# Four of the heaviest node tiles of a graph kernel change places with four light ones

## The chip, the core and the metric

The kernel runs on one core of one Trainium2 chip. The metric is device time in microseconds (us) of one execution. The engines are named as in the profile: PE (TensorE, matmul), DVE (VectorE), ACT (ScalarE), POOL (GpSimd, which here issues the indirect gathers) and SP (SyncE, which issues plain DMAs).

## What is computed

A graph of 6250 nodes with 256 features each and 100,000 edges passes through four residual layers. Cut to what matters:

```
x = x + relu(GAT(layernorm(x)))         # 8 heads; softmax over a node's incoming edges
x = x + relu(MoE32(layernorm(x)))       # one of 32 small experts for each node
x = x + segment_sum((layernorm(x) @ W[edge_type])[src] * edge_weight, dst)   # 16 relations
x = x + layernorm(mix of 2 of 8 experts(layernorm(x)) + layernorm(x))
```

The edges are sorted by destination, so a node's incoming edges stand together; their number is the node's degree. The largest degree in the inputs is 32.

## The kernel before

Nodes are worked in 49 tiles of 128. A tile's edges are fetched column by column: one indirect gather on POOL brings, for each of 128 nodes, the row of its j-th edge, so a tile needs as many gathers as the largest degree in it (and eight at least). To waste few of them, the first stage (`search_and_project`) sorts the nodes by degree: it counts them in bins of degree (L397 to L420), and from a node's rank its tile is `rank_high` (the rank divided by 128, L423) and its row in the tile is `rank_low` (L424). Tile 0 is the lightest and tile 48 the heaviest. All later stages take tiles in this order.

The number of gathers of each tile, from the degrees in the inputs:

| tiles | gathers each |
|---|---|
| 0 to 8 | 8, 9, 10, 11, 11, 11, 12, 12, 12 |
| 9 to 16 | 13, 13, 13, 13, 14, 14, 14, 14 |
| 17 to 26 | 15 (five times), 16 (five times) |
| 27 to 38 | 17 (five times), 18 (four times), 19 (three times) |
| 39 to 44 | 20, 20, 20, 21, 21, 22 |
| 45 to 48 | 22, 23, 25, 32 |

They add up to 799, once in each of two stages.

`attention` works tiles in pairs (2i, 2i+1); tile 48 is alone. For a tile, POOL gathers a window of edge keys (L788), the rows (L812) and the node's own record (L818). DVE makes a mask (L1176), waits until all gathers have landed, makes the scores (L1181 to L1186), and waits for ACT's exponentials (L855). Then it weighs and adds the rows, `items` steps of four columns (L1212 and L1217, with L1232 the last), and releases the buffer (`summed`). The row buffer holds 48 columns for two tiles of up to 32 each: POOL may begin tile t when tile t-2 is summed, and column 16 of tile t when tile t-1 is. PE works behind this: the small experts of pair i-2 and the relation projections of pair i-4. ACT works all of it in one written order (`pair`, from L931): it evacuates two projection chunks (L905, `tr_row`), makes the exponentials of the even tile, evacuates further chunks, does four of the eight expert steps (L896, `mo_ht`), makes the exponentials of the odd tile, and goes on. So whatever of PE's output comes behind a late exponential in this order waits for it.

`relations` gathers again (L1444), now rows of the projected table, and DVE adds them one column at a time in PSUM (L1639 and L1640, in steps of four columns) after it has released the next indices (L1649). Beside it PE works the eight dense experts of tiles 0 to 27 in seven groups of four, and the other 21 tiles are left to the last stage, `feed_forward`, which has no gathers and is alike for all tiles.

Of the kernel before, what the change touches and what calls it, by code (L numbers as in the profile page):

```python
# [16 lines left out]
F32 = mybir.dt.float32  # L17
BF16 = mybir.dt.bfloat16
I32 = mybir.dt.int32
U32 = mybir.dt.uint32  # L20
ALU = mybir.AluOpType
# [3 lines left out]
P = 128  # L25
N_NODES, N_EDGES, D = 6250, 100000, 256
NT = -(-N_NODES // P)
# [69 lines left out]
def spread(ap, axis, shape):  # L97

    return ap.unsqueeze(axis).broadcast_to(shape)
# [79 lines left out]
def search_and_project(p: Program):  # L179
# [3 lines left out]
    PARTS = U  # L183
    NEXT_AT, COUNT_AT, ORDER_AT = 27, 31, 37
    FIELDS = 3
    CELLS = DBINS * NT
    CB = CELLS // 4
    with p.phase() as ctx:
        def sb(n, s, d):
            return ctx.enter_context(nc.sbuf_tensor(n, s, d))  # L190
# [7 lines left out]
        chunk_i = sb("chunk_i", [P, NT], I32)  # L198
        shared = sb("shared", [P, NT * FIELDS * NT], F32)
        found = shared[:, 0:NT * P].bitcast(I32).rearrange("q (t e) -> q t e", e=P)  # L200
        valued = shared[:].rearrange("q (t f h) -> q t f h", f=FIELDS, h=NT)
        cmp = sb("cmp", [P, NT, P], BF16)
# [6 lines left out]
        ranked = sb("ranked", [P, DBINS, NT], F32)  # L209
        base = sb("base", [P, 4, DBINS], F32)  # L210
        rank = sb("rank", [P, NT], F32)
        rank_i, rank_high, rank_low = (sb(n, [P, NT], I32) for n in ("rank_i", "rank_high", "rank_low"))
        rank_row = sb("rank_row", [P, NT, HT - HROW], F32)
        fields = sb("fields", [P, NT, FIELDS], F32)
        hot_high = p.win[:].rearrange("q t c -> q (t c)")[:, 0:NT * NT].rearrange("q (t h) -> q t h", h=NT)
# [23 lines left out]
        high_ready, row_ready, low_ready, valued_ready, ordered = (  # L239
            p.sem(x) for x in ("high_ready", "row_ready", "low_ready", "valued_ready", "ordered"))  # L240
# [45 lines left out]
        def _(pool):  # L286
# [27 lines left out]
            for k in range(PARTS):  # L314
                lo, hi = k * U, (k + 1) * U
                pool.wait_ge(high_ready, k + 1)
                pool.tensor_tensor(valued[:, lo:hi], spread(hot_high[:, lo:hi, :], 2, [P, U, FIELDS, NT]),
                                   spread(fields[:, lo:hi, :], 3, [P, U, FIELDS, NT]), ALU.mult).then_inc(valued_ready, 1)

# [7 lines left out]
        def _(dve):  # L327
            chain = Chain(p, dve, steps_v)
# [89 lines left out]
            chain(ins)  # L418
            chain(dve.tensor_tensor(ranked[:], ranked[:], hot[:], ALU.mult))
            chain(dve.tensor_reduce(rank[:], ranked[:].rearrange("q b t -> q t b"), AX, ALU.add))  # L420
            dve.tensor_copy(rank_row[:, :, 0], rank[:]).then_inc(row_ready, 1)
            chain(dve.tensor_copy(rank_i[:], rank[:]))
            chain(dve.tensor_scalar(rank_high[:], rank_i[:], bits, None, ALU.arith_shift_right))  # L423
            chain(dve.tensor_scalar(rank_low[:], rank_i[:], P - 1, None, ALU.bitwise_and))  # L424

            for k in range(PARTS):
                lo, hi = k * U, (k + 1) * U
# [7 lines left out]
            dve.wait_ge(ordered, 1)  # L435
            chain(dve.tensor_copy(p.info[:].rearrange("q f t -> q (f t)"), p.bank[4][:, 0:FIELDS * NT]))
            dve.sem_inc(info_ready, 1)
# [1659 lines left out]
def build(nc, a):  # L2097
    with ExitStack() as ctx:
        p = Program(nc, ctx, a)
        search_and_project(p)  # L2100
        attention(p)
        p.rec = p.keep("rec", [P, max(DONE, TAIL), D], F32)
        relations(p)
        p.gb = p.keep("gb", [P, 2, D], F32)
        p.xd = [p.keep(f"xd{n}", [P, G, D], F32) for n in range(2)]
        p.x3 = [p.keep(f"x3{n}", [P, G, D], F32) for n in range(2)]
        choose_two(p)
        feed_forward(p)
# [33 lines left out]
```

## Time and profile before

| | us |
|---|---|
| median of 3 runs (3031.24 to 3037.5) | 3033.62 |
| the profiled execution's own time | 3030.64 |
| its span, first to last instruction | 3028.8 |
| PE busy | 2529.5 (84%) |
| POOL busy | 1947.3 (64%) |
| DVE busy | 1785.2 (59%) |
| ACT busy | 906.6 (30%) |

By the trace's order of instructions the stages lie about so: `search_and_project` to 141 us, `attention` from there to about 1788, `relations` from about 1793 to 2820, and the choice of two experts and `feed_forward` from there to the end. Shares of the whole span say little, since the stages have different limits; each is read by itself.

### The profile page before, as it was taken

To read this page: it belongs to the slowest core of one execution; us is meant where nothing else is said; L and a number is where in the kernel's file an instruction comes from. 1 tells how busy PE (TensorE), PEld (TensorE's weight loads), DVE (VectorE), ACT (ScalarE), POOL (GpSimd) and SP (SyncE) were. 2 spreads that over 40 slices of the span, in tenths; PEclk is the share of its full clock that TensorE was granted. 3 is DMA by queue.
4 is the path that set the end of the run, shared out by engine and by line. 5 is a ranking of instruction groups with operands and counts; after the bars stand their busy time and mean duration, and the time that the engine had idled before them with its cause. 6 is when DMAs were issued, how large, how long until landed. Compare 5 with 4: busy or idle time off the path is not lost. (4 is left out here: it accounts for less than half of the span.)

```text
span 3028.8 us, 39157 instructions
## 1 busy us (share of the span) xinstructions
PE 2529.5 (84%) x9508; PEld 1701.3 (56%) x9508; DVE 1785.2 (59%) x4152; ACT 906.6 (30%) x1799; POOL 1947.3 (64%) x1892
## 2 busy tenths in 40 slices
PE   4626999999999999998869953999999999940497
PEld 3515666666666666665546622666666666630265
DVE  6867665656566766666652016665556555444688
ACT  2312343334333433333223321333333333300321
POOL 6377746665667777787750027777777777776255
PEclk9858999999999999999989976999999999965699
DMA  7463545455545555555541265555556455443332
GB/s 247 115 191 93 149 143 150 137 157 151 152 141 165 163 157 156 164 171 153 153 123 70 82 218 183 152 156 156 150 155 184 143 147 150 142 121 99 123 123 69
DMA packets 257283, 443.01 MB, mean 146 GB/s; under 512 B 51178, under 2 KB 148066, under 8 KB 257186
## 3 DMA queue, kind: packets, MB, share of 16 engines
q0 software_dynamic: 84608, 232.41, 28.9%
q1 hardware_dynamic: 136626, 176.53, 16.9%
q10 hardware_dynamic: 35952, 33.04, 3.3%
q8 instruction: 29, 0.48, 0.1%
q14 instruction: 68, 0.56, 0.1%
HBM read 275.36 MB, written 166.45 MB: 146 GB/s over the span
## 5 line engine op out<-in xcount | busy, mean ns | idle before, releaser
L812 POOL DMA_INDIRECT gat_rows<-h_table,idx x799 | 902.9, 1130 | 374.9 <-issue 235.7
L1444 POOL DMA_INDIRECT rel_rows<-transformed,rel_idx x799 | 755.3, 945 | 468.0 <-issue 460.8
L1056 PE MATMUL bank<-tr_wr,tr_xt 128*128 128x512 f32 x1568 | 722.9, 601 | 51.1 <-ACT tr_row L905 46.2
L1056 PEld LDWEIGHTS bank<-tr_wr,tr_xt 128*128 128x128 f32 x1568 | 297.0, 192 | 334.0 <-issue 270.5
L905 ACT ACTIVATE tr_row<-bank 128x512 f32<-128x512 f32 x392 | 233.6, 597 | 661.5 <-PE bank L1056 636.2
L1499 PE MATMUL bank<-ex_xt,ex_w 128*128 128x512 f32 x896 | 420.2, 596 | 8.6 <-ACT ex_ht L1575 7.1
L1640 DVE SCALAR_TENSOR_TENSOR bank<-rel_rows,rel_now,bank 128x256 f32<-128x256 f32 x823 | 403.2, 490 | 40.3
L1021 PE MATMUL bank<-mo_xt,mo_w 128*128 128x256 f32 (+1 forms) x1600 | 408.9, 379 | 19.4 <-ACT mo_ht L896 17.7
L1508 PE MATMUL bank<-ex_w,ex_ht 128*128 128x256 f32 x1792 | 420.7, 380 | 0.0
L1508 PEld LDWEIGHTS bank<-ex_w,ex_ht 128*128 128x128 f32 x1792 | 341.6, 191 | 129.1 <-issue 93.6
L1039 PE MATMUL bank<-mo_w,mo_ht 128*128 128x256 f32 x1568 | 368.9, 381 | 5.3 <-ACT mo_ht L896 5.3
L1021 PEld LDWEIGHTS bank<-mo_xt,mo_w 128*128 128x128 f32 x1600 | 287.0, 193 | 111.3 <-issue 57.9
L1039 PEld LDWEIGHTS bank<-mo_w,mo_ht 128*128 128x128 f32 x1568 | 299.6, 191 | 55.5 <-issue 11.0
L1212 DVE TENSOR_TENSOR gat_rows<-gat_rows 128x1024 f32<-128x1024 f32 (+1 forms) x169 | 254.7, 1531 | 111.4 <-DVEq L1203 111.2
L1499 PEld LDWEIGHTS bank<-ex_xt,ex_w 128*128 128x128 f32 x896 | 171.1, 191 | 142.2 <-issue 121.3
L1575 ACT ACTIVATE ex_ht<-bank,ex_b 128x512 f32<-128x512 f32 x224 | 153.2, 686 | 275.6 <-ACTq L1574 275.6
L896 ACT ACTIVATE mo_ht<-bank,mo_b 128x256 f32<-128x256 f32 (+1 forms) x400 | 164.9, 464 | 229.2 <-PE bank L1021 198.2
L1217 DVE TENSOR_TENSOR gat_rows<-gat_rows 128x1056 f32<-128x1056 f32 x169 | 212.0, 1255 | 1.7
L1583 ACT ACTIVATE ex_y<-bank 128x256 f32<-128x256 f32 x224 | 85.8, 383 | 232.2 <-ACTq L1582 232.2
L1649 DVE CAST rel_idx<-win 128x32 int32 (+1 forms) x49 | 12.1, 246 | 216.2 <-DMA rel_rows<-transformed,rel_idx 213.2
L1532 PE MATMUL bank<-ms,rec 128*128 128x1 f32 x84 | 14.8, 308 | 137.3 <-DVEq L1723 97.9
L1181 DVE TENSOR_TENSOR gat_score<-gat_rows,gat_x 128x256 f32<-128x256 f32 x49 | 30.6, 625 | 140.7 <-DMA gat_rows<-h_table,idx 122.1
(296 smaller groups left out, 2252.4 us busy)
## 6 DMA issues: line engine op xcount, KB each, us to landing
transformed<-tr_row SPq DMA_DIRECT2D x392, 256.0 KB, 2.3
ys<-ex_y ACTq DMA_DIRECT2D x224, 128.0 KB, 2.0
gat_rows<-h_table,idx POOLq DMA_INDIRECT x799
rel_rows<-transformed,rel_idx POOLq DMA_INDIRECT x799
ex_w<-L_ffn_W SPq DMA_DIRECT2D x16, 512.0 KB, 12.1
ff_ye<-ys SPq DMA_DIRECT2D x14, 512.0 KB, 7.4
h_table<-hrow SPq DMA_DIRECT2D x49, 132.0 KB, 2.6
records<-xa SPq DMA_DIRECT2D x49, 132.0 KB
```

The source lines that it names most:

```text
L812: pool.indirect_dma_start(out=rows[:, column(u, j), :], out_offset=None, in_=p.h_table[:], in_offset=bass.IndirectOffsetOnAxis(ap=idx[u][: ...
L896: ins = act.activation(ht[:, b % HALF, 0:n * P], p.bank[2 + k % 2][:, h * PT:h * PT + n * P], ACT.Relu, bias=b1[:, b:b + 1])
L905: act.activation(trow[c % SLOTS_T][:], p.bank[6 + c % 2][:], ACT.Copy).then_inc(evacuated, 1)
L1021: ins = pe.matmul(to[h], w1[:, kd, b * P:(b + 1) * P], xt[:, kd, 0:n * P], start=(h == 0 and kd == 0), stop=(h == 1 and kd == KD - 1))
L1039: ins = pe.matmul(p.bank[4 + u][:, 0:D], ht[:, b % HALF, u * P:(u + 1) * P], w2[:, b, :], start=(b == 0), stop=False)
L1056: ins = pe.matmul(p.bank[6 + c % 2][:], xt2[:, k, u * P:(u + 1) * P], wr[:, k, m * CW:(m + 1) * CW], start=(k == 0), stop=(k == KD - 1))
L1212: dve.tensor_tensor(m[:, :, :, 0:HEAD_DIM], m[:, :, :, 0:HEAD_DIM], m[:, :, :, HEAD_DIM:HW].broadcast_to([P, COLS[s], HEADS, HEAD_DIM]), A ...
L1217: dve.tensor_tensor(total, total, columns(u, JCOL, 2 * JCOL) if s == 0 else part(s), ALU.add).then_inc(summing, 1)
L1444: pool.indirect_dma_start(out=rows[:, column(u, j), :], out_offset=None, in_=p.transformed[:], in_offset=bass.IndirectOffsetOnAxis(ap=idx[ ...
L1499: ins = pe.matmul(p.bank[3 + n % 2][:], w1[:, e, k, f * P:(f + 1) * P], xt[:, k, :], start=(k == 0), stop=(k == KD - 1))
L1508: ins = pe.matmul(p.bank[5 + m % 3][:, 0:D], ht[:, e % 2 * F + f, j * P:(j + 1) * P], w2[:, e * F + f, :], start=(f == 0), stop=(f == F - 1))
L1640: return dve.scalar_tensor_tensor(total, row, w, total, ALU.mult, ALU.add)
```

## The change

The tile number of a node is changed after the sort, so the node keeps its row in the tile. With `HEAVIEST` 4 and `SPREAD_AT` 9, tiles 45, 46, 47 and 48 change places with tiles 15, 13, 11 and 9: `step_` is 105 - 3h for tile number h; a heavy tile (h of 45 or more) moves by that, and a light one (odd, 9 to 15) by half of it. The odd member of pairs 4, 5, 6 and 7 is now a heavy tile. In the order of the program the gathers of each tile now are:

| tiles | before | after |
|---|---|---|
| 8, 9 | 12, 13 | 12, 32 |
| 10, 11 | 13, 13 | 13, 25 |
| 12, 13 | 13, 14 | 13, 23 |
| 14, 15 | 14, 14 | 14, 22 |
| 44, 45 | 22, 22 | 22, 14 |
| 46, 47 | 23, 25 | 14, 13 |
| 48 | 32 | 13 |

```diff
+    HEAVIEST, SPREAD_AT = 4, 9
...
-        rank_i, rank_high, rank_low = (sb(n, [P, NT], I32) for n in ("rank_i", "rank_high", "rank_low"))
+        rank_i, rank_high, rank_low, rank_odd = (sb(n, [P, NT], I32) for n in ("rank_i", "rank_high", "rank_low", "rank_odd"))
+        tile_at = sb("tile_at", [P, 4, NT], F32)
...
             chain(dve.tensor_reduce(rank[:], ranked[:].rearrange("q b t -> q t b"), AX, ALU.add))
-            dve.tensor_copy(rank_row[:, :, 0], rank[:]).then_inc(row_ready, 1)
             chain(dve.tensor_copy(rank_i[:], rank[:]))
             chain(dve.tensor_scalar(rank_high[:], rank_i[:], bits, None, ALU.arith_shift_right))
             chain(dve.tensor_scalar(rank_low[:], rank_i[:], P - 1, None, ALU.bitwise_and))
+            moved_to, step_, light, heavy = (tile_at[:, n, :] for n in range(4))
+            chain(dve.tensor_scalar(rank_odd[:], rank_high[:], 1, None, ALU.bitwise_and))
+            chain(dve.tensor_copy(moved_to, rank_high[:]))
+            chain(dve.tensor_scalar(step_, moved_to, -3.0, float(2 * NT + SPREAD_AT - 2), ALU.mult, ALU.add))
+            chain(dve.scalar_tensor_tensor(light, moved_to, float(SPREAD_AT), rank_odd[:], ALU.is_ge, ALU.mult))
+            chain(dve.scalar_tensor_tensor(light, moved_to, float(SPREAD_AT + 2 * HEAVIEST - 2), light, ALU.is_le, ALU.mult))
+            chain(dve.scalar_tensor_tensor(heavy, moved_to, float(NT - HEAVIEST), step_, ALU.is_ge, ALU.mult))
+            chain(dve.scalar_tensor_tensor(light, light, 0.5, step_, ALU.mult, ALU.mult))
+            chain(dve.tensor_tensor(moved_to, moved_to, light, ALU.add))
+            chain(dve.tensor_tensor(moved_to, moved_to, heavy, ALU.add))
+            chain(dve.tensor_copy(rank_high[:], moved_to))
+            chain(dve.scalar_tensor_tensor(rank[:], moved_to, float(P), rank_low[:], ALU.mult, ALU.add))
+            dve.tensor_copy(rank_row[:, :, 0], rank[:]).then_inc(row_ready, 1)
```

On DVE, at the end of the sort in the first stage, before the change (`ranked` and `rank` are the rank in float, `rank_row` its copy for the table that SP stores, `win` and `hot_low` the one-hot masks for PE, `xn` a normed tile of the projection):

```order
L419 TENSOR_TENSOR ranked<-ranked,hot 128x1568
L420 TENSOR_REDUCE rank<-ranked 128x49
L421 COPY rank_row<-rank 128x49
L422 CAST rank_i<-rank 128x49
L423 TENSOR_SCALAR rank_high<-rank_i 128x49
L424 TENSOR_SCALAR rank_low<-rank_i 128x49
L428 TENSOR_TENSOR win<-rank_high,count 128x343
L430 TENSOR_TENSOR hot_low<-rank_low,count 128x896
```

and after it, from the tile number on:

```order
L424 TENSOR_SCALAR rank_high<-rank_i 128x49
L425 TENSOR_SCALAR rank_low<-rank_i 128x49
L429 TENSOR_SCALAR rank_odd<-rank_high 128x49
L430 CAST tile_at<-rank_high 128x49
L431 TENSOR_SCALAR tile_at<-tile_at 128x49
L432 SCALAR_TENSOR_TENSOR tile_at<-tile_at,rank_odd 128x49
...
L438 CAST rank_high<-tile_at 128x49
L439 SCALAR_TENSOR_TENSOR rank<-tile_at,rank_low 128x49
L440 COPY rank_row<-rank 128x49
L444 TENSOR_TENSOR win<-rank_high,count 128x343
L446 TENSOR_TENSOR hot_low<-rank_low,count 128x896
```

Eleven small chained instructions have come between the tile number and the masks, and the copy to `rank_row` stands behind them. On PE, ACT, POOL and SP the rows are the same in both programs but for line numbers; there it is the loops' counts that change, since they are read from a table made on the chip. So for each tile in `attention`, POOL's rows stand as

```order
L788 DMA w_buf<-pairs,w_at 128x64
L804 REGISTER_ALU
L812 DMA gat_rows<-h_table,idx 128x268 x8
L818 DMA gat_x<-records,w_at 128x264
L583 COMPARE_AND_BRANCH
L812 DMA gat_rows<-h_table,idx 128x268
```

in both, with a branch and one further gather (L583, L812) for each column above eight, up to the tile's count. What moves is how often the last two repeat at a place, as the table says.

## Rows read from the trace of the kernel before

**Rows 1.** Busy time by engine (instructions), granted clock, DMA: the middle of `attention`.

```profile
core 0: us, PE busy (x) PEld busy (x) DVE busy (x) ACT busy (x) POOL busy (x), PEclk, DMA share, GB/s
286.00:1280.00 994.00, 991.87 (x3834) 668.90 (x3833) 628.68 (x1254) 358.03 (x690) 673.98 (x603) 1.00 0.52 151
```

**Rows 2.** Timeline of PE, end of `attention`: start, us, instructions, [idle before <-releaser].

```profile
1467.81 3.60 PE L1056 MATMUL bank<-tr_wr,tr_xt 128*128 128x512 f32 x8
...
1488.84 6.78 PE L1056 MATMUL bank<-tr_wr,tr_xt 128*128 128x512 f32 x8 [8.93 <-ACT tr_row L905]
...
1528.24 1.13 PE L1021 MATMUL bank<-mo_xt,mo_w 128*128 128x256 f32 x4 [1.14 <-ACT mo_ht L896]
...
1577.81 6.67 PE L1056 MATMUL bank<-tr_wr,tr_xt 128*128 128x512 f32 x8 [23.97 <-ACT tr_row L905]
```

**Rows 3.** Timeline of ACT: exponentials of tiles 9, 10, 11, 12, 46 and 47.

```profile
347.37 0.67 ACT L855 ACTIVATE gat_rows<-gat_score 128x256 f32<-128x256 f32 x1
...
380.94 0.67 ACT L855 ACTIVATE gat_rows<-gat_score 128x256 f32<-128x256 f32 x1 [0.49 <-issue]
...
407.49 0.67 ACT L855 ACTIVATE gat_rows<-gat_score 128x256 f32<-128x256 f32 x1 [0.19 <-issue]
...
440.86 0.67 ACT L855 ACTIVATE gat_rows<-gat_score 128x256 f32<-128x256 f32 x1 [0.44 <-issue]
...
1487.69 0.67 ACT L855 ACTIVATE gat_rows<-gat_score 128x256 f32<-128x256 f32 x1 [10.47 <-DVE gat_score L1186]
...
1526.93 0.67 ACT L855 ACTIVATE gat_rows<-gat_score 128x256 f32<-128x256 f32 x1 [10.30 <-DVE gat_score L1186]
```

**Rows 4.** POOL's gathers of L812 alone, one stretch per tile: tiles 9, 47, 48.

```profile
313.00:333.00 20.00, 13.75 (x13) 1.00 0.66 194
...
1484.40:1522.20 37.80, 28.16 (x25) 0.86 0.61 175
1523.60:1571.90 48.30, 36.45 (x32) 0.84 0.43 119
```

**Rows 5.** Timeline of DVE: end of tile 9, mask of 10, scores and end of 47.

```profile
357.46 0.43 DVE L1232 TENSOR_TENSOR gat_acc<-gat_rows 128x264 f32<-128x264 f32 x1
...
363.05 0.24 DVE L1176 TENSOR_SCALAR gat_mask<-gat_place,info 128x32 f32<-128x32 f32 x1 [2.10 <-issue]
...
1524.15 0.62 DVE L1181 TENSOR_TENSOR gat_score<-gat_rows,gat_x 128x256 f32<-128x256 f32 x1 [8.90 <-DMA gat_rows<-h_table,idx]
...
1544.54 0.51 DVE L1232 TENSOR_TENSOR gat_acc<-gat_rows 128x264 f32<-128x264 f32 x1
```

**Rows 6.** Timeline of POOL and DVE as DVE begins to weigh a tile's rows.

```profile
1452.86 0.94 POOL L812 DMA_INDIRECT gat_rows<-h_table,idx  x1 [0.30 <-issue]
...
1456.34 2.00 POOL L812 DMA_INDIRECT gat_rows<-h_table,idx  x1 [0.30 <-issue]
1457.44 1.22 DVE L1212 TENSOR_TENSOR gat_rows<-gat_rows 128x1024 f32<-128x1024 f32 x1
```

**Rows 7.** POOL's gathers of L1444 alone: tile 48 of `relations`, and the whole stage.

```profile
2755.40:2795.30 39.90, 30.23 (x32) 0.50 0.37 105
1793.50:2795.30 1001.80, 755.34 (x799) 0.90 0.52 155
```

**Rows 8.** Timeline of `relations`: a held gather; adds of tiles 11 and 48; tile 12's start.

```profile
1844.29 0.94 POOL L1444 DMA_INDIRECT rel_rows<-transformed,rel_idx  x1 [2.18 <-DVEq L1693]
...
1968.06 8.03 DVE L1640 SCALAR_TENSOR_TENSOR bank<-rel_rows,rel_now,bank 128x256 f32<-128x256 f32 x15
...
1985.53 0.19 DVE L1649 CAST rel_idx<-win 128x32 int32 x1 [0.29 <-DVE rel_now L1645]
...
2797.74 16.80 DVE L1640 SCALAR_TENSOR_TENSOR bank<-rel_rows,rel_now,bank 128x256 f32<-128x256 f32 x31
```

**Rows 9.** Timeline of DVE and PE where the tile numbers are made.

```profile
100.31 0.19 DVE L423 TENSOR_SCALAR rank_high<-rank_i 128x49 int32<-128x49 int32 x1
100.53 0.19 DVE L424 TENSOR_SCALAR rank_low<-rank_i 128x49 int32<-128x49 int32 x1
...
104.26 0.69 PE L490 MATMUL bank<-ident,xn 128*128 128x128 f32 x2 [6.14 <-DVE xn L372]
```

## The prediction, made before the changed kernel was run

> **What bounds the kernel now.** The columns of busy time over the whole span mix stages, so I read stretch by stretch, and only the three stages that the change reaches: the end of the sort, `attention` and `relations`.
>
> The middle of `attention` belongs to PE. In 994 us PE is busy for 991.9, at the full granted clock (1.00, the 2.4 GHz level), while POOL's gathers fill 674 [rows 1]. A pair of tiles takes 60 us there: the exponentials of tiles 10 and 12 stand at 380.9 and 440.9, and ACT meets them without waiting for DVE [rows 3]. So a gather may come later there at no cost until ACT has to wait for it, and PE behind ACT.
>
> The end of `attention` belongs to POOL. A gather costs about 1.25 us from start to start (39.9 us for 32 where nothing disturbs it) [rows 7]; the stretches of tiles 47 and 48 take 37.8 and 48.3 us [rows 4], so with their windows and records pairs 23 and 24 need far more than 60 us of POOL. What ends PE's idle time there is ACT, and ACT waits for the scores: 10.47 us before the exponentials of tile 46, 10.30 before those of tile 47 [rows 3]. PE loses 8.93, 1.14 and 23.97 us [rows 2].
>
> `relations` belongs to POOL all along: 799 gathers in 1001.8 us, that is 1.25 each from the first to the last, with almost nothing between [rows 7]. PE's dense experts end long before it does (the last two stretches run at the lower clock). Here the order of tiles can't shorten the gathers, only make or remove waits between them and change what follows the last one.
>
> **The change, part by part.** *Longer sort.* Eleven chained DVE instructions come in front of the masks, of the size of those beside them, which start 0.22 us apart [rows 9]: 11 x 0.22 = +2.4 us. No cover: PE waits 6.14 us for DVE right behind [rows 9]. The copy to `rank_row` only changes place, and SP asks for it only behind tile 38 of the projection, whose `xn` DVE makes after the masks. Tiles and rows are otherwise the same, so all plain DMAs and matmuls are too.
>
> *The end of attention.* Tiles 45 to 48 now have 14, 14, 13 and 13 gathers. With 1.25 us each, plus window, record and a few slowed ones, a pair needs some 40 us of POOL, under the 60 of PE, as today's pairs 5 to 8 do, for which ACT doesn't wait [rows 3]. So the idle time behind tiles 46, 47 and 48 goes: 8.93 + 1.14 + 23.97 = 34.0. PE's first eight matmuls after the two long waits take 6.78 and 6.67 us where such a group takes 3.60 [rows 2]; those 3.2 and 3.1 go too. Together -40.3 us. Waits behind tiles up to 44 stay, since those tiles keep their gathers and so POOL its lateness.
>
> *The middle of attention.* Now heavy tiles stand in pairs 4 to 7, and I follow lateness through them. Two prices first. For an odd tile PE has work in hand when ACT stops: behind tile 47 ACT waited 10.30 us [rows 3] and PE lost 1.14 [rows 2], so 9.2 us are covered. For an even tile hardly any: behind tile 46 ACT waited 10.47 and PE lost 8.93 and 3.2 by slower matmuls, the wait plus 1.6.
>
> - Tile 9, 32 gathers for 13. Its gathers start at 313.0 and end at 333.0 [rows 4]; nineteen more at 1.25 end at about 356.6. From there to the scores it is 2 us (1522.2 to 1524.15 for tile 47) [rows 4, 5], and scores to exponentials take 2.8 (1524.15 to 1526.93) [rows 3, 5]: 361.4. ACT is there at 347.4, so it waits 14.0, and PE loses 14.0 - 9.2 = 4.8. Bounds: 0 if the stretch were shortened by more overlap, 9.7 if it took tile 48's whole 48.3 us.
> - Tile 10. DVE weighs tile 9 in seven steps; tile 47 with six took 18.1 us from exponentials to the end of L1232 (1526.93 to 1545.05) [rows 3, 5], so 18.1 x 7/6 = 21.1, ending at 382.5. Mask 5.2 later (357.89 to 363.05) [rows 5], exponentials 3.2 after the mask: 390.9. ACT, shifted by 4.8, is there at 380.45 + 4.8 = 385.2 [rows 3]. It waits 5.6, and PE loses 5.6 + 1.6 = 7.2.
> - Tile 11, 25 gathers, may start when tile 9 is summed, 383.4; with tile 47's 37.8 us [rows 4] its exponentials are ready at 383.4 + 37.8 + 4.8 = 426.0. ACT is there at 407.3 + 12.0 = 419.3, waits 6.7, under the 9.2: no loss.
> - Tile 12: 426.0 + 18.1 + 5.2 + 3.2 = 452.5, against ACT at 440.4 + 12.0 = 452.4: none. Tile 13 with 23 gathers starts at 445 and needs two gathers fewer than tile 47, so its exponentials are ready at 445 + 35.3 + 4.8 = 485.1; ACT is there 26.5 us behind tile 12, as at tiles 10 and 11, at 479: a wait of 6, no loss. Pairs 7 and on have regained their time.
>
> Together +12.0 us. Ends: 5 if PE's work in hand covers all of tile 9 and part of tile 10, and 29 if that stock isn't refilled after the first stall, so that tiles 11 and 13 cost their 6.7 and 6 too and tile 9's gathers take the upper bound.
>
> One row bears on the gathers' price. A gather that runs while DVE weighs rows takes 2.00 us instead of 0.94 [rows 6], so tile 47's stretch is longer than 25 x 1.25; the heavy tiles of the middle meet the short weighing of light neighbours, so I took today's stretch of tile 9 plus undisturbed gathers. The Trainium skill ("SBUF — State Buffer", section "Who interferes with whom") says that a `tensor_tensor` with two SBUF inputs contends only with GpSimd's reads and infers that descriptor generation isn't held up by it. By that a gather beside L1212 would stay at 0.94, tile 9's 33 issues would take some 41 us (an estimate from that page and 1.25 us each) and the whole come out 2 us lower; the row differs, and the sum goes by the row.
>
> *Relations.* The gathers keep their total. New waits: tile t may start when t-2 is summed, and a light even tile is now too short to cover a heavy odd one. Tile 9: from its last gather to DVE's adds 2.4 us (2795.3 to 2797.7) [rows 7, 8], 31 adds 16.8 us, then 2.2 until POOL goes on (a held gather waited 2.18) [rows 8], 21.4; tile 10's 13 gathers cover 16.3: POOL waits 5.1. Tile 11: 27 adds at 0.54, in all 19.2 against 16.3: 2.9. Tiles 13 and 15: 17.1 against 17.5: none. Sum +8.0. After the last gather tile 48 now has 15 adds instead of 31: 16 x 0.54 = -8.7. But DVE will begin them some 2 us later than today: it needs 9.4 us from the last add of an odd tile to the next even one (1976.1 to 1985.5) [rows 8], so with 2.4 + 8.1 us for tile 47 it is ready 19.9 us behind that tile's last gather, while 13 gathers take 16.3: the adds begin 3.6 + 0.6 instead of 2.4 behind the last gather, +1.8. In all +1.1 us; the ends are -7 (waits hidden) and +8 (no gain at the end).
>
> **Sum:** +2.4 - 40.3 + 12.0 + 1.1 = -24.8 us on the profiled execution's 3030.6, 3005.8. The median lies 3.0 us above that execution; on it, 3033.6 - 24.8 = 3008.8.
>
> **Rivals.** *More is hidden in the middle* (5 for 12, with relations at its lower end): -24.8 - 7 - 7, from 2995 to 3002. For it: POOL has about a third of the middle free [rows 1]. Against: that time can't be used ahead, since POOL may be only one tile in front of DVE.
>
> *PE's stock isn't refilled*: 29 for 12, so 3026, between 3019 and 3031. For it: the waits of tiles 11 and 13, 6.7 and 6, lie near the 9.2. Against: ACT is busy for 358 of 994 us where PE is full [rows 1], so it works about three times as fast as PE feeds it and catches up within a few steps.
>
> *Slower: the extra gathers aren't hidden at all.* Pairs 4 to 7 get 19 + 12 + 9 + 8 = 48 more gathers, 60 us. If each stands in front of ACT as at the end of the stage today, +60 takes the place of +12: 3033.6 + 2.4 - 40.3 + 60 + 1.1 = 3057. It decides against the change from 37 us of loss in these four pairs. For it: they come right behind the stage's start-up, with no lead. Against: by the steps above the second two heavy tiles find ACT late anyway.
>
> *The change doesn't move the tiles*: only the eleven instructions remain, 3036. The arithmetic of the new tile numbers gives whole numbers and the pairs listed, so hardly likely.
>
> **How the numbers follow.** Forecast 0.62, more hidden 0.12, stock not refilled 0.16, slower 0.07, not moved 0.03. The forecast's time is 3009. Eight in ten: from 2997, the middle of the better case, to 3024, which takes in the upper price of tile 9 and much of the third case. About 0.2% (6 us) is what a measurement of this kernel can tell from no change, so faster means under 3027.5: 0.62 + 0.12 + two thirds of 0.16, 0.84; within 0.2%: the rest of the third case and the last, 0.09; slower 0.07.
>
> **What would show it.** In the changed trace, POOL's stretches of 32 and 25 gathers stand at about 315 and 385 us. PE's timeline has idle time of about 5 us behind `mo_ht` at 360 and about 6 behind `tr_row` at 390, none over 2 us until tile 40, and none over 2 us behind the last four tiles. In `relations` POOL waits once for about 5 and once for about 3 us near tiles 11 and 13, and the last run of adds has 15. It is wrong if ACT waits over 15 us before tile 11 or 13, if PE still idles behind the last tiles (then it is DVE, not POOL, that is late there), or if gathers in the middle cost clearly more than 1.25 us.

## The result, and the profile after

| | before | after |
|---|---|---|
| median of 4 runs each, side by side | 3035.25 (3031.24 to 3037.5) | 3016.08 (3015.09 to 3017.26) |
| the profiled execution, its span | 3030.64, 3028.8 | 3016.06, 3014.2 |

The ratio is 0.9934, with a 95% interval of 0.9922 to 0.9946: the change makes the kernel 0.7% faster. The forecast was 3009.

Where the time went stands in the start times of a few rows of each trace: the first gather of `attention`, the exponentials of tiles 26 and 44, the first and the last gather of `relations`, the end of the router's matmuls (L1532 of before). The columns are the stretches between them, in us. The two columns "again" are second profiles of the same two kernels, from the experiments; two profiles of one kernel differ by 3 to 5 us in all, so a difference of 1 or 2 us in a stretch says nothing.

| stretch | before | before again | after | after again | predicted change |
|---|---|---|---|---|---|
| to the first gather of `attention` | 146.5 | 145.2 | 149.3 | 147.5 | +2.4 |
| to tile 26's exponentials (middle) | 714.4 | 716.0 | 730.6 | 730.2 | +12.0 |
| to tile 44's exponentials | 554.3 | 555.4 | 555.9 | 555.7 | 0 |
| to the first gather of `relations` (end of `attention`) | 378.4 | 378.4 | 337.2 | 337.2 | -40.3 |
| gathers of `relations` | 1001.6 | 1002.6 | 1014.5 | 1012.2 | +8.0 |
| from the last gather to the router's end | 25.7 | 25.6 | 17.5 | 17.5 | -6.9 |
| to the end | 207.9 | 208.8 | 209.1 | 208.8 | 0 |
| span | 3028.8 | 3032.0 | 3014.2 | 3009.0 | -24.8 |

**End of the sort.** PE's row of after that answers to [rows 9] (timeline: start, length, instructions, idle before and who ended it):

```profile
107.09 0.69 PE L506 MATMUL bank<-ident,xn 128*128 128x128 f32 x2 [8.75 <-DVE xn L374]
```

The wait has grown by 2.6 and the row stands 2.8 later.

**End of `attention`.** Busy time of the stretch (PE, PEld, DVE, ACT, POOL, then clock), and ACT's exponentials of tiles 46, 47 and 48 of after, which answer to [rows 2] and [rows 3]:

```profile
1480.00:1768.00 288.00, 278.45 (x1021) 174.47 (x1020) 66.32 (x158) 104.24 (x199) 32.51 (x31) 0.99 0.30 102
```

```profile
1498.32 0.67 ACT L871 ACTIVATE gat_rows<-gat_score 128x256 f32<-128x256 f32 x1 [0.46 <-issue]
1524.90 0.67 ACT L871 ACTIVATE gat_rows<-gat_score 128x256 f32<-128x256 f32 x1 [0.18 <-issue]
1558.12 0.68 ACT L871 ACTIVATE gat_rows<-gat_score 128x256 f32<-128x256 f32 x1 [0.28 <-issue]
```

Waits of 10.47 and 10.30 us before the exponentials are gone; ACT meets the scores ready. PE's 8.93, 1.14 and 23.97 have no row in after.

**Middle of `attention`.** The same stretch as [rows 1], 2.8 later, and a short one of PE alone behind its first wait (busy, clock, DMA share, GB/s):

```profile
288.80:1282.80 994.00, 981.99 (x3775) 659.84 (x3776) 650.05 (x1269) 353.36 (x684) 738.33 (x638) 0.99 0.54 156
```

```profile
366.00:372.00 6.00, 5.46 (x14) 0.50 0.50 159
```

PE was busy for 991.87 of 994 before and is for 981.99 now, with 59 instructions fewer in the same time. The idle time has grown by only 10 us, from 2 to 12, and for 6 us the matmuls ran at the 1.2 GHz level (0.50). PE's timeline of after shows both:

```profile
355.77 1.03 PE L1037 MATMUL bank<-mo_xt,mo_w 128*128 128x256 f32 x4
...
366.54 2.08 PE L1037 MATMUL bank<-mo_xt,mo_w 128*128 128x256 f32 x4 [5.21 <-ACT mo_ht L912]
...
376.78 1.88 PE L1072 MATMUL bank<-tr_wr,tr_xt 128*128 128x512 f32 x4
...
395.54 3.70 PE L1072 MATMUL bank<-tr_wr,tr_xt 128*128 128x512 f32 x8 [0.62 <-ACT tr_row L921]
400.24 0.28 PE L1018 MATMUL bank<-mo_identb,mo_hot 128*128 128x128 bf16 x2 [1.00 <-DVE mo_hot L1144]
401.65 2.53 PE L1072 MATMUL bank<-tr_wr,tr_xt 128*128 128x512 f32 x4 [1.12 <-ACT tr_row L921]
...
407.36 1.88 PE L1072 MATMUL bank<-tr_wr,tr_xt 128*128 128x512 f32 x4
...
464.75 1.98 PE L1072 MATMUL bank<-tr_wr,tr_xt 128*128 128x512 f32 x4 [0.97 <-ACT tr_row L921]
467.60 1.13 PE L1037 MATMUL bank<-mo_xt,mo_w 128*128 128x256 f32 x4 [0.86 <-ACT mo_ones L902]
...
469.64 1.88 PE L1072 MATMUL bank<-tr_wr,tr_xt 128*128 128x512 f32 x4
```

The group that starts at 366.54 takes 2.08 us where the same group before the wait took 1.03. To see what all this costs, I count PE's matmuls of a line and take the same ones in before. Four of the rows above (355.77, 376.78, 407.36, 469.64) are these of before:

```profile
352.25 1.02 PE L1021 MATMUL bank<-mo_xt,mo_w 128*128 128x256 f32 x4
...
364.98 1.88 PE L1056 MATMUL bank<-tr_wr,tr_xt 128*128 128x512 f32 x4
...
390.23 1.88 PE L1056 MATMUL bank<-tr_wr,tr_xt 128*128 128x512 f32 x4
...
450.21 1.88 PE L1056 MATMUL bank<-tr_wr,tr_xt 128*128 128x512 f32 x4
```

PE is late by 3.5 us ahead of tile 9's wait, 11.8 behind it, 17.1 behind tile 10's, 19.4 behind tile 12's, and stays there: a matmul near 600 us is also 19.4 late. So tile 9 costs 8.3, tile 10 5.3, tiles 11 and 12 2.3, and the rest nothing: 15.9 in all. The sum holds in the second profile of after, but its parts move. By the same count it is 15.4 there, of which tile 9 costs 5.9, tile 10 5.5 and tile 12 4.0. Tile 9's row is this one:

```profile
363.57 2.08 PE L1037 MATMUL bank<-mo_xt,mo_w 128*128 128x256 f32 x4 [4.11 <-ACT mo_ht L912]
```

PE came to this wait 1.9 us less late than in the first profile, tile 9's exponentials stood 3.0 us earlier, and the clock was back sooner (0.94 between 366 and 372 us).

ACT in the same stretch: the exponentials of tiles 9, 10, 11 and 12 (L871), and two evacuations (L921) that wait for something else:

```profile
365.23 0.67 ACT L871 ACTIVATE gat_rows<-gat_score 128x256 f32<-128x256 f32 x1 [14.38 <-DVE gat_score L1202]
...
394.23 0.68 ACT L871 ACTIVATE gat_rows<-gat_score 128x256 f32<-128x256 f32 x1 [1.99 <-DVE gat_score L1202]
...
401.00 0.60 ACT L921 ACTIVATE tr_row<-bank 128x512 f32<-128x512 f32 x1 [5.03 <-DMA transformed<-tr_row]
...
430.79 0.68 ACT L871 ACTIVATE gat_rows<-gat_score 128x256 f32<-128x256 f32 x1 [6.36 <-DVE gat_score L1202]
...
457.75 0.68 ACT L871 ACTIVATE gat_rows<-gat_score 128x256 f32<-128x256 f32 x1 [0.20 <-issue]
...
464.10 0.60 ACT L921 ACTIVATE tr_row<-bank 128x512 f32<-128x512 f32 x1 [3.12 <-DMA transformed<-tr_row]
```

ACT waits 5.03 and 3.12 us not for scores but for a store of an earlier chunk to leave its buffer. SP issues the x store of pair i-3 (L781) in front of the chunk stores of pair i-4 (L787), and the x store waits for DVE; when DVE is late with a heavy tile, ACT's four `tr_row` buffers are held through SP's queue. SP's timeline has no chunk store between 387.25 and 398.19:

```profile
397.40 0.42 SPq L781 DMA_DIRECT2D x_moved<-tr_x  x1
398.19 12.37 SPq L787 DMA_DIRECT2D transformed<-tr_row  x8
```

A late DVE also reaches PE directly, by the one-hot mask `mo_hot` (1.00 at 400.24).

**`relations`.** All gathers as one stretch (POOL busy, clock, DMA share, GB/s), POOL's three longest waits between gathers that before does not have, and DVE's last run of adds:

```profile
1773.00:2787.60 1014.60, 758.31 (x799) 0.89 0.52 153
```

```profile
1957.86 0.95 POOL L1460 DMA_INDIRECT rel_rows<-transformed,rel_idx  x1 [5.16 <-DVEq L1709]
2008.42 0.95 POOL L1460 DMA_INDIRECT rel_rows<-transformed,rel_idx  x1 [3.21 <-DVEq L1709]
2319.05 0.95 POOL L1460 DMA_INDIRECT rel_rows<-transformed,rel_idx  x1 [2.38 <-issue]
...
2790.45 8.03 DVE L1656 SCALAR_TENSOR_TENSOR bank<-rel_rows,rel_now,bank 128x256 f32<-128x256 f32 x15
```

Against [rows 7] the gathers take 12.8 more: two waits for DVE (5.16 and 3.21, less the usual 0.30 each), 7.8; one of 2.1 that waits for nothing in the profile, at the second gather of tile 28; and 3.0 because a gather took 949 ns on the mean instead of 945. The last run of adds has 15 and starts 2.9 us behind the last gather's end (2787.6), where it was 2.5 before.

### The profile page after: what moved, and what is told of

The parts are those of the page before. It is cut to its first block and busy times, and to the rows that moved or that the text cites. A ratio compares the mean times of both kernels' runs of the same rounds, so it can differ in the third digit from the quotient of the medians.

```text
span 3014.2 us, 39170 instructions
## 1 busy us (share of the span) xinstructions
PE 2536.2 (84%) x9508; PEld 1702.3 (56%) x9508; DVE 1784.8 (59%) x4163; ACT 907.8 (30%) x1799; POOL 1972.8 (65%) x1892
## 5 line engine op out<-in xcount | busy, mean ns | idle before, releaser
L828 POOL DMA_INDIRECT gat_rows<-h_table,idx x799 | 917.3, 1148 | 307.3 <-issue 240.0
L1037 PE MATMUL bank<-mo_xt,mo_w 128*128 128x256 f32 (+1 forms) x1600 | 416.3, 384 | 22.1 <-ACT mo_ht L912 19.4
L921 ACT ACTIVATE tr_row<-bank 128x512 f32<-128x512 f32 x392 | 233.9, 598 | 662.5 <-PE bank L1072 632.3
L1656 DVE SCALAR_TENSOR_TENSOR bank<-rel_rows,rel_now,bank 128x256 f32<-128x256 f32 x823 | 403.2, 490 | 40.3
L1228 DVE TENSOR_TENSOR gat_rows<-gat_rows 128x1024 f32<-128x1024 f32 (+1 forms) x169 | 254.5, 1530 | 87.7 <-DVEq L1219 87.7
L1233 DVE TENSOR_TENSOR gat_rows<-gat_rows 128x1056 f32<-128x1056 f32 x169 | 211.7, 1252 | 1.7
L1665 DVE CAST rel_idx<-win 128x32 int32 (+1 forms) x49 | 11.8, 241 | 224.0 <-DMA rel_rows<-transformed,rel_idx 221.2
L1197 DVE TENSOR_TENSOR gat_score<-gat_rows,gat_x 128x256 f32<-128x256 f32 x49 | 30.6, 625 | 145.2 <-DMA gat_rows<-h_table,idx 127.0
## 6 DMA issues: line engine op xcount, KB each, us to landing
ex_w<-L_ffn_W SPq DMA_DIRECT2D x16, 512.0 KB, 11.4
```

The costliest lines, as they stand in the source:

```text
L828: pool.indirect_dma_start(out=rows[:, column(u, j), :], out_offset=None, in_=p.h_table[:], in_offset=bass.IndirectOffsetOnAxis(ap=idx[u][: ...
L921: act.activation(trow[c % SLOTS_T][:], p.bank[6 + c % 2][:], ACT.Copy).then_inc(evacuated, 1)
L1037: ins = pe.matmul(to[h], w1[:, kd, b * P:(b + 1) * P], xt[:, kd, 0:n * P], start=(h == 0 and kd == 0), stop=(h == 1 and kd == KD - 1))
L1228: dve.tensor_tensor(m[:, :, :, 0:HEAD_DIM], m[:, :, :, 0:HEAD_DIM], m[:, :, :, HEAD_DIM:HW].broadcast_to([P, COLS[s], HEADS, HEAD_DIM]), A ...
L1233: dve.tensor_tensor(total, total, columns(u, JCOL, 2 * JCOL) if s == 0 else part(s), ALU.add).then_inc(summing, 1)
L1656: return dve.scalar_tensor_tensor(total, row, w, total, ALU.mult, ALU.add)
```

## The experiments

**The change without its effect, and before once more.** In `sort_only` the eleven instructions run but no tile moves; `before_again` is the unchanged kernel.

```diff
-            chain(dve.scalar_tensor_tensor(light, moved_to, float(SPREAD_AT), rank_odd[:], ALU.is_ge, ALU.mult))
+            chain(dve.scalar_tensor_tensor(light, moved_to, float(2 * NT), rank_odd[:], ALU.is_ge, ALU.mult))
...
-            chain(dve.scalar_tensor_tensor(heavy, moved_to, float(NT - HEAVIEST), step_, ALU.is_ge, ALU.mult))
+            chain(dve.scalar_tensor_tensor(heavy, moved_to, float(2 * NT), step_, ALU.is_ge, ALU.mult))
```

> The eleven instructions stay, but their bounds are set so that no tile is moved. Theory A (they stand uncovered in front of the masks): the profiled span is 2.4 to 2.8 us above before, first gather of attention at 149 instead of 146.5, all else as before. Rival (the sort is covered, or moving instructions there costs more than they take): under 1 or over 5 us.

> The kernel before, unchanged, for a second profile of it. Theory A (the two profiles differ only by the change): span within 3 us of 3028.8, 799 gathers of relations in 1001 to 1003 us, no gather of the end of that stage held by POOL itself. Theory B (part of the missing 5 us is the chip or the run, not the change): the 799 gathers take 1004 us or more here too, since in the changed kernel each was some 0.004 us slower and one wait of 2 us stood in POOL's own queue.

`sort_only` took 3035.65 against 3032.56 of before beside it (ratio 1.0008, 0.9999 to 1.0017). By the times alone that is not clear of noise, but the same matmul of PE as above stands at 106.51, 2.3 later than in before, with a wait of 8.76, and the gathers of `relations` take 1001.9. `before_again` had a span of 3032.0, its gathers took 1002.6, and none was held by POOL itself, as theory A said. So the instructions cost their 2 to 3 us, and everything else in the result comes from where the tiles stand.

**One heavy tile alone.** Only tiles 48 and 9 change places.

```diff
-    HEAVIEST, SPREAD_AT = 4, 9
+    HEAVIEST, SPREAD_AT = 1, 9
```

> HEAVIEST 1: only tiles 48 and 9 change places. Theory A (the price in the middle is made by the first heavy tile, behind which all later ones are late): the middle loses 11 of the 15 us that four heavy tiles cost (5 to 6 behind tile 9, some 5 behind tile 10), the end keeps PE's waits of 9 and 1 us behind tiles 46 and 47 and loses that of 24; with -3 in relations about 16 us under before. Rival (each heavy tile costs its share, about 4 us): 22 to 24 us under before.

It took 3028.63, only 4 us under before (ratio 0.9986, 0.9977 to 0.9996): a miss for both theories. Shown are PE's wait behind tile 46, POOL's last 16 gathers in `relations`, and DVE's adds of tiles 47 and 48:

```profile
1505.14 6.60 PE L1072 MATMUL bank<-tr_wr,tr_xt 128*128 128x512 f32 x8 [9.59 <-ACT tr_row L921]
```

```profile
2773.00:2792.60 19.60, 14.97 (x16) 0.50 0.38 107
```

```profile
2778.94 14.60 DVE L1656 SCALAR_TENSOR_TENSOR bank<-rel_rows,rel_now,bank 128x256 f32<-128x256 f32 x27
...
2801.93 8.03 DVE L1656 SCALAR_TENSOR_TENSOR bank<-rel_rows,rel_now,bank 128x256 f32<-128x256 f32 x15
```

The end of `attention` became 26 us shorter and the middle 10 to 11 longer, so one tile at place 9 costs over two thirds of what four cost. But the wait behind tile 46 stays (9.59). And in `relations` the last gathers end at 2792.6 while the last run of adds starts at 2801.93: DVE's adds for tile 47 with its 25 columns end only at 2793.54, and what it does between an odd tile and the next comes behind them. So the 16 adds fewer shorten nothing much (24.0 us from the last gather to the router's end, 25.6 before), while the gathers take 1009.2. In all `relations` lost some 5 us where theory A had put a gain of 3. The gain behind the last gather needs a light tile 47 as well as a light tile 48.

**Other places.** `spread17` puts the four heavy tiles at 17, 19, 21 and 23, further from the start-up of the stage; `even16` at 16, 18, 20 and 22, so that the heavy tile is the first of its pair.

```diff
-    HEAVIEST, SPREAD_AT = 4, 9
+    HEAVIEST, SPREAD_AT = 4, 17
```

```diff
-    HEAVIEST, SPREAD_AT = 4, 9
+    HEAVIEST, SPREAD_AT = 4, 16
...
-            chain(dve.scalar_tensor_tensor(light, moved_to, float(SPREAD_AT), rank_odd[:], ALU.is_ge, ALU.mult))
+            chain(dve.scalar_tensor_tensor(light, moved_to, float(SPREAD_AT), rank_odd[:], ALU.is_ge, ALU.is_gt))
```

> SPREAD_AT 17: the same four heavy tiles, now at 17, 19, 21 and 23, where POOL has waits of its own and ACT meets scores that are long ready. Theory A (the price in the middle comes of standing right behind the start-up, where POOL has no lead): PE has no idle time over 2 us in the middle, attention 41 us shorter at its end, relations with one wait of 2 us, in all about 40 us under before, 18 to 22 under the changed kernel. Rival (a heavy tile beside a light one costs the same at any place): 15 to 22 us under before, as the changed kernel.

> The four heavy tiles at 16, 18, 20 and 22, the even members of their pairs, one place before those of spread17 (17, 19, 21, 23). Theory C (at 17 to 23 the price comes through DVE: the second half of a heavy odd tile's gathers waits until the light even tile is summed, its weighing takes 20 us, and the next even tile's scores, for which PE has hardly any work in hand, come late; a heavy even tile is followed by an odd one, for which PE has 9 us in hand): the middle loses 2 to 6 us instead of about 20, and the whole is 12 to 18 us under spread17, near 2995. Rival (a pair of heavy and light costs the same in either order): as spread17, 3011.

`spread17` took 3011.1 (0.9931, 0.9917 to 0.9944), `even16` 3007.47 (0.992, 0.9903 to 0.9937). Their middles are 735.4 and 734.8 us long, even a little longer than that of after; they regain it in `relations`, where one longer wait of POOL, 2.73 and 2.92 us, stands in place of two of 5.16 and 3.21 (gathers 1006.1 and 1006.2). So neither a place further on nor the order in a pair makes the heavy tiles free; I had expected both to. ACT's exponentials of tiles 17 to 20 in `spread17` show what goes on:

```profile
598.67 0.67 ACT L871 ACTIVATE gat_rows<-gat_score 128x256 f32<-128x256 f32 x1 [9.13 <-DVE gat_score L1202]
628.22 0.67 ACT L871 ACTIVATE gat_rows<-gat_score 128x256 f32<-128x256 f32 x1 [5.33 <-DVE gat_score L1202]
665.38 0.68 ACT L871 ACTIVATE gat_rows<-gat_score 128x256 f32<-128x256 f32 x1 [8.23 <-DVE gat_score L1202]
694.06 0.67 ACT L871 ACTIVATE gat_rows<-gat_score 128x256 f32<-128x256 f32 x1 [3.79 <-DVE gat_score L1202]
```

PE's loss by the count above is 20.9 us there: 7.6 by tiles 17 and 18, the rest behind tiles 20, 22 and 24. I read this as each heavy tile finding POOL and DVE still late from the one before; the next run tests it.

**A light pair between heavy ones.** `odd_spaced` puts them at 17, 21, 25 and 29, one to every second pair (one DVE instruction more).

```diff
-    HEAVIEST, SPREAD_AT = 4, 9
+    HEAVIEST, SPREAD_AT = 4, 17
...
-            chain(dve.tensor_scalar(rank_odd[:], rank_high[:], 1, None, ALU.bitwise_and))
+            chain(dve.tensor_scalar(rank_odd[:], rank_high[:], 3, None, ALU.bitwise_and))
+            chain(dve.tensor_scalar(rank_odd[:], rank_odd[:], 1.0, None, ALU.is_equal))
...
-            chain(dve.tensor_scalar(step_, moved_to, -3.0, float(2 * NT + SPREAD_AT - 2), ALU.mult, ALU.add))
+            chain(dve.tensor_scalar(step_, moved_to, -5.0, float(4 * (NT - 1) + SPREAD_AT), ALU.mult, ALU.add))
...
-            chain(dve.scalar_tensor_tensor(light, moved_to, float(SPREAD_AT + 2 * HEAVIEST - 2), light, ALU.is_le, ALU.mult))
+            chain(dve.scalar_tensor_tensor(light, moved_to, float(SPREAD_AT + 4 * HEAVIEST - 4), light, ALU.is_le, ALU.mult))
...
-            chain(dve.scalar_tensor_tensor(light, light, 0.5, step_, ALU.mult, ALU.mult))
+            chain(dve.scalar_tensor_tensor(light, light, 0.25, step_, ALU.mult, ALU.mult))
```

> The four heavy tiles at 17, 21, 25 and 29: still odd, but with an untouched pair between (one more small DVE instruction in the sort, 0.2 us). Theory C1 (DVE's lateness adds up over neighbouring pairs, and one light pair is enough to make it good): only the tile with 32 gathers costs, some 7 us, and the whole is 10 to 13 us under spread17. Rival C2 (each heavy odd tile costs by itself): as spread17 within 4 us.

It took 2998.31 (0.9893, 0.9876 to 0.9909), some 13 us less than after and than `spread17`, as the theory said. ACT's exponentials of tiles 17 to 20, to be read against those of `spread17`, and PE's rows behind tiles 17 and 18:

```profile
598.18 0.67 ACT L872 ACTIVATE gat_rows<-gat_score 128x256 f32<-128x256 f32 x1 [9.70 <-DVE gat_score L1203]
627.69 0.67 ACT L872 ACTIVATE gat_rows<-gat_score 128x256 f32<-128x256 f32 x1 [5.29 <-DVE gat_score L1203]
656.99 0.68 ACT L872 ACTIVATE gat_rows<-gat_score 128x256 f32<-128x256 f32 x1 [0.18 <-issue]
690.13 0.67 ACT L872 ACTIVATE gat_rows<-gat_score 128x256 f32<-128x256 f32 x1 [0.21 <-issue]
```

```profile
599.49 1.13 PE L1038 MATMUL bank<-mo_xt,mo_w 128*128 128x256 f32 x4 [0.54 <-ACT mo_ht L913]
628.84 5.40 PE L1073 MATMUL bank<-tr_wr,tr_xt 128*128 128x512 f32 x8 [3.75 <-ACT tr_row L922]
635.97 1.98 PE L1073 MATMUL bank<-tr_wr,tr_xt 128*128 128x512 f32 x4 [1.62 <-ACT tr_row L922]
```

The tile with 32 gathers costs 8.3 us of PE's time, nearly all behind the light tile that follows it; then the lateness is gone, and the tiles with 25, 23 and 22 gathers cost nothing. The middle is 722.5 us long, and the gathers of `relations` take 1004.6, with one wait of POOL behind the heaviest tile (2.75 us before tile 19) and none behind the others.

The light pair is worth the 12.9 us by which the middle is shorter than that of `spread17` (735.4). Against after the middle is only 8 us shorter, and 3 are lost again up to tile 44; another 8 to 10 us come from the gathers of `relations`, of which `spread17` has 6 to 8 already by its places (1006.1).

**The order of SP's stores.** `after_again` is the changed kernel unaltered, beside `store_later`, which issues the chunk stores in front of the x store:

```diff
             def pair(i):
-                store(i - 3)
                 store_chunks(i - 4)
+                store(i - 3)
```

> The changed kernel, with SP's store of a pair's new x put behind the chunk stores of the older pair instead of in front of them. In the profile the x store waits for DVE's finish, and the chunk stores behind it keep ACT's four chunk buffers, 5.0 us at 396 and 3.1 at 461. Theory D (this is a second way by which a late DVE holds PE, beside the exponentials): ACT's waits for the chunk stores behind tiles 10, 12, 40, 42 and 44 fall under 1 us, and the whole is 4 to 8 us under the changed kernel. Rival (what waits there is released by the exponentials in any case): within 2 us of it.

> The changed kernel, unchanged, on the chip of the other runs of this call: 0.6 to 0.7% under before; its gathers of relations show whether the 13 us more than before (8 of them waits) come again. Chip or run: within 1010 us for the 799 gathers. The change: 1013 to 1016 us.

`after_again` took 3011.8 (0.9939, 0.9922 to 0.9956), `store_later` 3009.15 (0.9927, 0.991 to 0.9943). The difference of 2.7 us lies within the intervals, under theory D's 4 to 8. `after_again` repeats the longer gathers of `relations` (1012.2). PE's rows of `store_later` that answer to those of after from 366 to 470 us:

```profile
363.77 1.13 PE L1037 MATMUL bank<-mo_xt,mo_w 128*128 128x256 f32 x4 [2.75 <-ACT mo_ht L912]
...
392.75 5.39 PE L1072 MATMUL bank<-tr_wr,tr_xt 128*128 128x512 f32 x8 [3.38 <-ACT tr_row L921]
...
456.13 3.70 PE L1072 MATMUL bank<-tr_wr,tr_xt 128*128 128x512 f32 x8 [1.44 <-ACT tr_row L921]
460.97 0.28 PE L1018 MATMUL bank<-mo_identb,mo_hot 128*128 128x128 bf16 x2 [1.14 <-DVE mo_hot L1144]
```

ACT has no wait for a chunk store left there, and PE's loss in the middle, counted as above, is 11.4 instead of 15.4 to 15.9. But that is hardly the store order's doing. Tile 9 costs 2.9 us here, all of it idle time, where it cost 5.9 in `after_again`; no chunk store is waited for ahead of it in either, and PE simply came to it 1.5 us later. Tile 10 costs 5.5 in both, and tile 12 3.0 instead of 4.0. The wait for late scores grows in place of the other (3.38 where 0.62 and, in `after_again`, 1.89 stood), and behind tile 12 PE waits for `mo_hot` (1.14). So the queue does hold ACT, but what it held back is late by DVE's other ways too: as far as these runs show, the rival is right.

**More of it.** `spaced_six` spreads the six heaviest tiles as `odd_spaced` does four (the edit is against `odd_spaced`); `spaced_store` is `odd_spaced` with the order of `store_later`; `spaced_six_store` has both.

```diff
-    HEAVIEST, SPREAD_AT = 4, 17
+    HEAVIEST, SPREAD_AT = 6, 17
```

> The change with the six heaviest tiles (43 to 48) in places 17, 21, 25, 29, 33 and 37, one to every second pair: tile 48 to place 17, tile 47 to 21, and so on down to tile 43 in place 37. Theory (a place costs only where it gets many more gathers than its neighbours and has no light pair behind it; the end costs because heavy tiles stand in neighbouring pairs): places 33 and 37 get 5 and 3 more gathers each and cost nothing, and in the last pairs PE's wait of 6.3 us that odd_spaced still has at 1430 us goes, with its slow matmuls; waits at 1293 and 1360 stay, since tiles 40 to 42 keep their gathers. So 7 us under odd_spaced, 2991, with the stretch from tile 44's exponentials to the first gather of relations unchanged. Rival (each tile moved into the middle takes from PE's stock what it gives back at the end): within 3 us of odd_spaced, 2995 to 3001, with new waits of PE behind tiles 33 to 40.

> odd_spaced with SP's order of store_later: the projection chunks go into SP's queue ahead of the x store. Theory D (a late DVE holds ACT's tr_row buffers over SP's queue): the chunks wait behind the x store only where DVE is late, behind place 17 and at the end of the stage, so it gives 1 to 3 us under odd_spaced, 2995 to 2997. Rival (the waits only merge with those behind the late exponentials): no difference over 1 us, 2998.

> Both of the above. If they act at different places, the sum of both: spaced_six less 1 to 3 us, 2988 to 2990. If the order of the stores only counts where DVE is late, it gives less here than in spaced_store, under 1 us, since fewer late tiles are left at the end.

`spaced_six` took 3001.82 (0.9905, 0.9889 to 0.9922), `spaced_store` 2996.5 (0.9883, 0.9866 to 0.9899), `spaced_six_store` 3001.23 (0.9905, 0.9888 to 0.9921). These runs were timed beside other runs of before than `odd_spaced`, so the ratios are compared. The last two heavy tiles bring nothing (0.9905 against 0.9893, with intervals that overlap), as the rival said: PE's wait of 6.25 us at 1430 in `odd_spaced` is gone, but others have come, behind place 37 for instance:

```profile
1236.26 3.70 PE L1073 MATMUL bank<-tr_wr,tr_xt 128*128 128x512 f32 x8 [2.10 <-ACT tr_row L922]
```

ACT waits 4.05 and 3.64 us there before the exponentials of tiles 37 and 38, with 21 gathers in place 37, only two more than stood there (place 33 gets four more; I had written 5 and 3). That a light pair regains less among neighbours of 18 or 19 gathers than among those of 15 would explain it, but was not tried by itself. The store order takes ACT's waits for chunk stores out of `spaced_store` too, 6.05 us behind tile 18 among them, but what is left of that in the ratio, 0.1%, is less than the intervals span; with six tiles nothing is left of it. `odd_spaced` and `spaced_store` are the fastest kernels here, 1.1 to 1.2% under before, and not told apart.

## Why the prediction was right, and where it missed

The forecast of 3009 lies 7 us under the median of 3016.08, 1.6 of them because before itself took 3035.25 this time and not 3033.6. The sign of each stage is as it said, and its size within 4 us. By its own steps:

- *Sort*, +2.4: +2.8 and +2.3 in the two pairs of profiles. Right.
- *End of `attention`*, -40.3: -41.2, twice. Right, with its mechanism: POOL's pairs fit under PE's, and the slow matmuls behind the long waits go as well.
- *Middle*, +12.0: 15.9 and 15.4. This term was mis-sized, and it came as near as this because its errors went both ways.
  - Tile 9: 8.3 and 5.9 for 4.8. ACT's wait of 14.0 was 14.38, and PE's work in hand covered 9.2 of it, as forecast (5.21 idle). But I priced only the idle time. The matmuls behind it ran at the 1.2 GHz level and cost 3.1 more (8.3 less 5.21), 1.8 in the second profile (5.9 less 4.11). The price for an odd tile came from tile 47 of before, whose 1.14 us of idle time had no slow matmuls behind it [rows 2]; I had counted them for even tiles alone. How much idle time there is depends on where PE stands when the wait begins, and that moves by some 2 us from profile to profile.
  - Tile 10: 5.3 and 5.5 for 7.2. ACT waited for the scores for 1.99 us instead of 5.6, since it came later than I had it. By my price that would be 3.6; the rest came with the wait of 5.03 for a chunk store, a way from the late DVE to ACT that I had not followed.
  - Tiles 11 and 12: 2.3 and 4.0 for none. ACT's wait at tile 11 was the 6.7 forecast (6.36), covered. Behind tile 12 the scores came in time, as forecast, but SP's queue held `tr_row`. In `store_later`, where it doesn't, tile 12 costs 3.0 by late scores and a late `mo_hot`: what I put at nothing is DVE's lateness, by whichever way it comes.
  - Tile 13 and on: none, as forecast.
- *Relations*, +1.1: the second profiles give +1.5 (1012.2 + 17.5 against 1002.6 + 25.6), the first +4.7. The two waits came to 4.9 and 2.9 where 5.1 and 2.9 stood. The wait of 2.1 us in POOL's own queue comes again: at the same gather it is 2.35 long (with the usual 0.30) in the second profile and 2.40 in `store_later`, and neither profile of before has it. The 3.0 us by slower gathers are in the first profile alone. Both stay unexplained. Of the 1.8 us for a late DVE at the end, 0.4 came.

Against the second profiles the sum of -24.8 stands beside -23.0 (3032.0 to 3009.0), against the first beside -14.6; by the medians it is -19.2 in the first comparison and -18.6 in the second. About 4 us of the miss is thus the middle, shown above; the rest is spread over stretches that differ as much between two profiles of one kernel, and is left open.

Of the rivals, *stock not refilled* did not come: the waits of tiles 11 and 13 (6.36 and 4.03) were covered in full. *More is hidden* was false for these places; `odd_spaced` reaches its time, 2998. What I didn't see is that the four places were the change's weak point. At places 17 to 23 neighbouring pairs share one lateness, and a light pair between them takes 13 us off the middle; place 17 instead of 9 takes another 6 to 8 us off the gathers of `relations`. At place 9 a light pair alone was not tried; it could save little, since one heavy tile there cost 11.5 of the 15.4 to 15.9.

## What to carry to other kernels

Heavy items spread over a pipeline with slack are hidden best if each is worked off before the next comes: with four heavy tiles in neighbouring pairs the kernel gained 0.7%, with a light pair between them 1.1%. When a wait is priced, add the slower matmuls behind it to the idle time, and follow a late engine along every way on which something waits for it, the stores' too; closing one of them gained nothing clear here, because the same lateness came by the others. In a stage that sums at its end, the last two tiles count together, since the engine that sums them is behind by one.

## What the runs showed of the hardware

A gather of tile 10 that POOL issues while DVE weighs the heavy tile 9 takes 2.00 us instead of 0.95, and a heavy tile keeps that up for seven issues in a row. DVE's and POOL's timelines of after:

```profile
366.66 3.43 DVE L1228 TENSOR_TENSOR gat_rows<-gat_rows 128x2048 f32<-128x2048 f32 x2
```

```profile
367.15 2.62 POOL L828 DMA_INDIRECT gat_rows<-h_table,idx  x1 [0.30 <-DVE idx L1212]
370.07 2.00 POOL L828 DMA_INDIRECT gat_rows<-h_table,idx  x1 [0.30 <-issue]
...
387.69 1.07 POOL L804 DMA_INDIRECT w_buf<-pairs,w_at  x1 [0.30 <-issue]
```

Over the whole trace of after, the 132 gathers of `attention` that lie almost wholly beside DVE's weighing (L1228, L1233) have a median of 2.00 us, and the 606 that touch none of it 0.95. From tile 10's first gather (362.03) to the next tile's window it takes 25.7 us; before it took 21.9 (334.35 to 356.22). So the weighing of a long tile stretches the gathers of the tile behind it by some 4 us, which the forecast had left out. Here it cost little: tile 10's scores waited for DVE's own mask, and from tile 9's exponentials to tile 11's it was 65.6 us, where the forecast had 64.6. The Trainium skill ("SBUF — State Buffer", section "Who interferes with whom") infers that a `tensor_tensor` does not hold descriptor generation up; these rows differ again, as [rows 6] did.
